# First attention of a two-layer macaron block: the own values' first block in three rounded passes instead of one fp32 product, with some products at the start and end of the stage put in another order

## The reference, cut to what matters

```python
x = x + 0.5 * ffn0(layernorm(x))
x = x + attn0(layernorm(x))            # the stage that is changed
x = x + 0.5 * ffn0(layernorm(x))
x = x + 0.5 * ffn1(layernorm(x)); x = x + attn1(layernorm(x)); x = x + 0.5 * ffn1(layernorm(x))

# attn0: 32 query heads of 128, 8 shared key/value heads, and 32 "latent" keys and values of their own
q  = rope(x @ w_q);  k = rope(x @ w_k) # k, v: one for each group of 4 query heads
v  = x @ w_v
lk = rope((x @ w_lq) @ w_lk);  lv = x @ w_lv     # one for each query head
attn = softmax(mask(q k^T / sqrt(128))) v        # over the shared keys
lat  = softmax(mask(q lk^T / sqrt(128))) lv      # over the head's own keys
return attn @ w_o + lat @ w_lo
```

## Time and profile before

| what | us |
|---|---|
| median of 3 runs | 1792.02 (1790.3 to 1793.99) |
| the profiled execution | 1789.53 |
| its span, first to last instruction | 1787.7 |
| PE busy | 1726.3 (97%) |
| DVE busy | 1169.4 (65%) |
| ACT busy | 1075.1 (60%) |
| POOL busy | 916.4 (51%) |
| first attention, about | 92 to 1347 |
| one group of 16 steps inside it | 154.3 |
| own product: L1141 and L1143 busy | 77.1 and 49.1 |

### The profile page before, as it was taken

One profiled execution on the slowest core, in us unless ns is written; L12 is line 12 of the kernel. 1 busy time (PEld: TensorE's weight loads), 2 busy tenths in 40 slices (PEclk: granted clock), 3 DMA queues, 4 the chain that ended last, 5 costly groups with the idle time before them and its releaser, 6 DMA issues.

```text
span 1787.7 us, 32013 instructions
## 1 busy us (share of the span) xinstructions
PE 1726.3 (97%) x10988; PEld 1501.7 (84%) x10988; DVE 1169.4 (65%) x3498; ACT 1075.1 (60%) x3013; POOL 916.4 (51%) x1169
## 2 busy tenths in 40 slices
PE   7989999999999999999999999999999998899798
PEld 6788999998998999899899899989878776677567
DVE  6675566566557656755665665676566676888756
ACT  3356656566656666655665664666553264888964
POOL 4555545455544555554555554545532255877850
PEclk9999999999999999999999999999999999999999
DMA  4300011012001101200110110020021121000101
GB/s 145 110 24 13 15 58 42 1 42 61 13 19 54 42 1 48 65 1 19 56 40 1 60 54 1 19 72 24 1 65 54 42 59 48 2 2 2 42 7 48
DMA packets 35424, 65.77 MB, mean 37 GB/s; under 512 B 4032, under 2 KB 4672, under 8 KB 35264
## 3 DMA queue, kind: packets, MB, share of 16 engines
q1 hardware_dynamic: 35264, 63.73, 11.6%
HBM read 61.62 MB, written 2.10 MB: 36 GB/s over the span
## 4 chain that ended last, share of the span: by engine, by line
PE 69%; ACT 11%; DVE 10%; issue 6%; POOL 3%; DMA 1%; SPq 0%; DVEq 0%; POOLq 0%; ACTq 0%
PE bank L367 57%; PE bank L1118 4%; ACT s L1264 2%; PE bank L1141 2%; PE bank L1752 2%; ACT W L263 1%; PE bank L1143 1%; DVE h L765 1%; PE bank L1723 1%; DVE work L1376 1%; DVE W L269 1%; ACT s L1818 1%; DVE work L1367 1%; PE bank L1739 1%; ACT qk L1255 1%
## 5 line engine op out<-in xcount | busy, mean ns | idle before, releaser
L1505 POOL TENSOR_TENSOR qk<-work,qk 128x512 fp32r<-128x512 f32 (+1 forms) x160 | 188.7, 1179 | 474.8 <-ACT qk L1255 474.7
L1497 POOL TENSOR_TENSOR work<-work,table 128x512 f32<-128x512 f32 (+1 forms) x160 | 190.0, 1187 | 110.5 <-ACT work L1250 110.4
L1264 ACT ACTIVATE s<-s,neg_max 128x128 f32<-128x128 f32 (+1 forms) x512 | 228.0, 447 | 1.9 <-DVE neg_max L1390 1.9
L1271 ACT CAST pt_pair<-bank 128x384 fp32r<-128x384 f32 x128 | 61.8, 482 | 249.3 <-PE bank L1118 249.3
L367 PE MATMUL bank<-W,o_own 128*128 128x512 f32 x768 | 200.6, 396 | 0.0
L1255 ACT CAST qk<-work 128x512 fp32r<-128x512 f32 (+1 forms) x160 | 92.5, 578 | 178.9 <-DVE work L1376 178.9
L367 PE MATMUL bank<-W,xnA 128*128 128x320 f32 (+1 forms) x1056 | 195.5, 339 | 3.4 <-DVE xnA L352 2.6
L367 PE MATMUL bank<-W,o_pair 128*128 128x512 f32 x768 | 197.5, 399 | 0.0
L1367 DVE TENSOR_TENSOR work<-bank,table 128x512 f32<-128x512 f32 (+1 forms) x160 | 101.9, 637 | 130.6 <-ACT work L1250 128.7
L367 PEld LDWEIGHTS bank<-W,xnA 128*128 128x128 f32 x1056 | 166.1, 189 | 17.6 <-DVE xnA L352 3.7
L367 PE MATMUL bank<-qk 128*128 128x256 f32 (+1 forms) x768 | 166.1, 352 | 0.9 <-POOL qk L1505 0.9
(11 more groups left out here) (124 smaller groups left out, 3801.9 us busy)
## 6 DMA issues: line engine op xcount, KB each, us to landing
raw<-in_weights SPq DMA_DIRECT2D x215, 256.0 KB, 2.7
x<-in_x SPq DMA_DIRECT2D x8, 256.0 KB, 6.1
out<-x SPq DMA_DIRECT2D x8, 256.0 KB, 2.0
row<-in_bias_rows SPq DMA_DIRECT2D x5, 256.0 KB, 2.9
table<-in_constants SPq DMA_DIRECT2D x4, 240.0 KB, 3.2
b_qk<-in_bias_rows SPq DMA_DIRECT2D x1, 512.0 KB, 3.9
b_val<-in_bias_rows SPq DMA_DIRECT2D x1, 256.0 KB, 3.0
table<-in_constants SPq DMA_DIRECT2D x1, 66.0 KB, 2.5
```

Source lines behind the costliest of these rows:

```text
L1264: last = nc.scalar.activation(s0[:, s, cols], s0[:, s, cols], ACT.Exp, bias=neg_max[:, s, qt:qt + 1], scale=-1.0, accum_out=row_sum[:, s, ...
L1271: nc.scalar.copy(pt_pair[HI][:, before.h % 2, :, :].rearrange("p b q -> p (b q)"), bank[PT][:, 0:3 * P]).then_inc(a_pt_hi, 1)
L1497: nc.gpsimd.tensor_tensor(work[:, s, cols], work[:, s, cols], table[:, T_SIN + cols.start:T_SIN + cols.stop], ALU.mult).then_inc(a_sin, 1)
L1505: nc.gpsimd.tensor_tensor(lo, work[:, 2 + s, st.columns(what)], hi.bitcast(F32), ALU.subtract).then_inc(a_rope_lo, 1)
```

## The change

1. The values and the weights of the first key block (256 columns of `pt_own`, the first token tile of the own values) are now held as HI and LO parts (`v_front`, `pt_front`) and multiplied by `product` in three fp32r passes. The second block (128 columns) stays one fp32 matmul (`v_rear`, `pt_rear`).
2. ACT's one copy of 384 columns becomes a cast of 256 (`pt_front` HI) and a copy of 128 (`pt_rear`); DVE gets a new instruction, `turned_own_lo`, that makes the LO part of `pt_front` and only then raises `a_pt_own`.
3. On DVE the values of the first token tile are cast and subtracted for all 640 columns instead of being copied for 512 and split for 128.
4. `v_rear` is the tile `row`, so SP's load of the bias row waits for X2, the end of the attention, and with it what stands behind it in the queue.
5. On PE the second half of the latent query projection (`other_half`: 12 products of 512 columns) goes ahead of the own product in step 1; in the last group, steps 14 to 16, `output` products go ahead of `weigh_pair` and of `turn(1)`.

```diff
@@ -171,10 +171,12 @@
                 qk = [sb(s, f"qk{i}", [P, 6, SEQ], F32R) for i in (HI, LO)]
-                lvv = sb(s, "lvv", [P, 2, GH * HD])
-                vs = [sb(s, f"vs{i}", [P, 2, HD], F32R) for i in (HI, LO)]
+                v_front = [sb(s, f"v_front{i}", [P, LVW], F32R) for i in (HI, LO)]
+                v_rear = row
+                vs_rear = [sb(s, f"vs_rear{i}", [P, HD], F32R) for i in (HI, LO)]
                 pt_pair = [sb(s, f"pt_pair{i}", [P, 2, 3, P], F32R) for i in (HI, LO)]
-                pt_own = sb(s, "pt_own", [P, 3 * P])
+                pt_front = [sb(s, f"pt_front{i}", [P, 2 * P], F32R) for i in (HI, LO)]
+                pt_rear = sb(s, "pt_rear", [P, P])
                 o_pair = [sb(s, f"o_pair{i}", [P, 2, SEQ], F32R) for i in (HI, LO)]
...
@@ -1044,8 +1047,8 @@
             turn_tiles((4, 5))
-            a0_run(pe, lambda st: a0_tensor_step(pe, st, lambda: turn_tiles((6, 7))), lambda: None,
-                   other_half)
+            a0_run(pe, lambda st: a0_tensor_step(pe, st, lambda: turn_tiles((6, 7)), other_half),
+                   lambda: None, lambda: None)
 
...
@@ -1138,9 +1141,9 @@
 
-                nc.tensor.matmul(bank[OB][:, 0:SEQ], lvv[:, 0, col:col + P], pt_own[:, 0:2 * P],
-                                 start=True, stop=False)
-                nc.tensor.matmul(bank[OB][:, P:SEQ], lvv[:, 1, col:col + P], pt_own[:, 2 * P:3 * P],
+                product(bank[OB][:, 0:SEQ], lambda p: v_front[p][:, col:col + P],
+                        lambda p: pt_front[p][:, :], True, False)
+                nc.tensor.matmul(bank[OB][:, P:SEQ], v_rear[:, col:col + P], pt_rear[:, :],
                                  start=False, stop=True).then_inc(a_pv_own, 1)
@@ -1173,22 +1176,28 @@
                 output(0, st.near(-3))
+            if not st.queries and st.h in (0, 2):
+                output(1, st.near(-2))
             if lag1 and before.paired():
                 weigh_pair()
                 turn(1)
             if st.queries and not st.first:
                 a0_queries(pe, st)
+            if not st.queries and st.h == 3:
+                output(0, st.near(-3))
             if lag1 and not before.paired():
                 turn(1)
+            if st.second and not st.first:
+                latent()
             for t in next_norms(st):
                 if t == 0:
                     pe.wait_ge(a_proj_free, st.near(-1).fill("q")[0] + 3)
                 ln_turn(pe, 16 + t, t, t % 2, normed, banks=2)
-            if lag2 and st.h in (1, 3):
+            if lag2 and (st.h == 1 or st.h == 3 and st.queries):
                 output(0, st.near(-3))
             if lag2 and st.h == 1:
                 output(0, st.near(-2))
-            if lag2 and st.h != 1:
+            if lag2 and (st.h == 3 or st.h != 1 and st.queries):
                 output(1, st.near(-2))
@@ -1273,7 +1282,8 @@
                 act.wait_ge(a_turned, before.inst(1)[0] + 1)
-                nc.scalar.copy(pt_own[:, :], bank[PT][:, 0:3 * P]).then_inc(a_pt_own, 1)
+                nc.scalar.copy(pt_front[HI][:, :], bank[PT][:, 0:2 * P])
+                nc.scalar.copy(pt_rear[:, :], bank[PT][:, 2 * P:3 * P]).then_inc(a_own_pt_hi, 1)
 
@@ -1403,6 +1413,11 @@
 
+            def turned_own_lo():
+                dve.wait_ge(a_own_pt_hi, before.number() + 1)
+                nc.vector.tensor_tensor(pt_front[LO][:, :], bank[PT][:, 0:2 * P], pt_front[HI][:, :].bitcast(F32),
+                                        ALU.subtract).then_inc(a_pt_own, 1)
+
             def pair_lo():
@@ -1419,16 +1434,23 @@
                 dve.wait_ge(a_proj, f + 1)
-                if half == 0:
-                    nc.vector.tensor_copy(lvv[:, tt, 0:HALF], bank[fs][:, 0:HALF]).then_inc(a_proj_free, 1)
-                    return
                 own = GH * HD - HALF
-                shared = bank[fs][:, own:HALF]
-                nc.vector.tensor_copy(vs[HI][:, tt, :], shared).then_inc(a_v_hi, 1)
-                nc.vector.tensor_copy(lvv[:, tt, HALF:GH * HD], bank[fs][:, 0:own])
-                dve.wait_ge(a_v_hi, st.values_before() + tt + 1)
-                nc.vector.tensor_tensor(vs[LO][:, tt, :], shared, vs[HI][:, tt, :].bitcast(F32),
-                                        ALU.subtract).then_inc(a_proj_free, 1)
+                if tt == 0:
+                    cols = slice(half * HALF, (half + 1) * HALF)
+                    hi, lo = [v_front[p][:, cols] for p in (HI, LO)]
+                    nc.vector.tensor_copy(hi, bank[fs][:, 0:HALF]).then_inc(a_v_hi, 1)
+                    dve.wait_ge(a_v_hi, st.values_before() + half + 1)
+                    nc.vector.tensor_tensor(lo, bank[fs][:, 0:HALF], hi.bitcast(F32),
+                                            ALU.subtract).then_inc(a_proj_free, 1)
+                elif half == 0:
+                    nc.vector.tensor_copy(v_rear[:, 0:HALF], bank[fs][:, 0:HALF]).then_inc(a_proj_free, 1)
+                else:
+                    shared = bank[fs][:, own:HALF]
+                    nc.vector.tensor_copy(vs_rear[HI][:, :], shared).then_inc(a_v_hi, 1)
+                    nc.vector.tensor_copy(v_rear[:, HALF:GH * HD], bank[fs][:, 0:own])
+                    dve.wait_ge(a_v_hi, st.values_before() + 3)
+                    nc.vector.tensor_tensor(vs_rear[LO][:, :], shared, vs_rear[HI][:, :].bitcast(F32),
+                                            ALU.subtract).then_inc(a_proj_free, 1)
 
@@ -1450,6 +1472,8 @@
                 inverses(1)
+            if lagging(st):
+                turned_own_lo()
             for t in next_applied(st):
@@ -2135,7 +2159,7 @@
                 st_tail.load(sp, j, flat(W_F1 - len(TAIL) + j))
-            sp.wait_ge(x_written, X1)
+            sp.wait_ge(x_written, X2)
             sp.dma_start(row[:, :], rows_in[0]).then_inc(row_loaded, 16)
```

More of the change, by code:

```diff
@@ L907, in program @@
         a_pt_own = sem("a_pt_own")
+        a_own_pt_hi = sem("a_own_pt_hi")
         a_pt_hi = sem("a_pt_hi")
@@ L946, in values_before @@
             def values_before(self):
-                return 2 * (self.g * BATCH + self.batch)
+                return 3 * (self.g * BATCH + self.batch)
             def paired(self):
@@ L1093, in score_columns, with a0_tensor_step @@
             return bank[2 + qt][:, (1 - k) * n:(2 - k) * n]
-        def a0_tensor_step(pe, st, between):
+        def a0_tensor_step(pe, st, between, latent):
             def scores():
@@ L1125, in weigh_pair @@
                 to = bank[OB][:, :].rearrange("p (e q) -> p e q", e=2)
-                product(to, lambda p: vs[p][:, 0, :],
+                product(to, lambda p: v_front[p][:, GH * HD:LVW],
                         lambda p: pt_pair[p][:, :, 0:2, :].rearrange("p e b q -> p e (b q)"), True, False)
-                product(to[:, :, P:SEQ], lambda p: vs[p][:, 1, :],
+                product(to[:, :, P:SEQ], lambda p: vs_rear[p][:, :],
                         lambda p: pt_pair[p][:, :, 2, :], False, True).then_inc(a_pv_pair, 1)
```

## The result

| | us |
|---|---|
| before, median of 6 | 1792.53 |
| after, median of 6 | 1799.32 (1796.72 to 1799.96) |
| ratio, 95% interval | 1.0037 (1.0025 to 1.0048) |
| profiled execution (span) before, after | 1789.53 (1787.7), 1798.65 (1796.9) |

It is slower by 6.8 us; the forecast was 1795.3, 2.8 slower on the median and 3.3 on the profiled pair, where 9.2 were found. The sign and the places are as forecast, the size is not.

What follows compares the result with a forecast made beforehand. PE, busy 97% of the span, was taken to bound the kernel. Regular groups +4.7, last group +1.0, start -1.9, end -0.5 gave +3.3 us: 1792.8 profiled, 1795.3 on the median; range 1790 to 1799, 8 in 10 1784 to 1802.

Steps and rivals of the forecast that it cites:

- The sign: Whole kernel against the kernel before: slower had a chance of 0.40, same 0.38, faster 0.22.
- this account: The main forecast for the whole kernel, 1795.3 on the median, chance 0.55, its own range 1790 to 1799.
- PE saves 0.07 a head: Own product's 256 columns on PE: three fp32r passes take 0.36 instead of 0.43 us, saving 1.12 per group.
- `a_pt_own` comes 0.53 later; waits at positions 2, 6, 10, 13 and 14: Own product's operand comes later; the five positions cost 0.64, 0.28, 0.27, 0.35 and 0.48 us in a regular group.
- my own three terms, 0.10, 0.03 and 0.42: Delay of `a_pt_own`: ACT ends 0.10 later, DVE needs 0.03 to see it and 0.42 us to subtract.
- Key steps: the rotation comes 0.69 later: DVE at positions 1, 5, 9, 13: subtraction ahead of the keys' rotation delays it 0.69 us and pushes later heads.
- Last group +1.0: Last group: normalisation stands behind the subtraction and positions 8 to 10 lack slack; +1.0 us, between 0.5 and 2.
- Start -1.9: Step 1: 12 latent products fill PE's idle time, 2.4 us shorter, about 0.5 eaten by positions 1 and 2.
- The larger work on the values: DVE's 320-column subtractions fall where DVE waits for PE: nothing, at most 0.5 us per sequence, 16.
- End -0.5, row 0: Moved output products give -0.5 us, between +0.5 and -3.6; the later row load costs nothing unless landing takes twice as long.
- "Passes simply saved": Rival, chance 0.20: in the regular groups the waits hide and PE's saving is kept, 1779 to 1783 us.
- "New step dearer": Rival, chance 0.18: ACT's copies don't overlap, subtraction meets POOL, `a_pt_own` comes 0.75 later; 1808 us, half way 1802.

Runs made afterwards that it cites:

- wait_only: Kernel before, own product still fp32, with ACT's copy in two pieces and an unused subtraction on DVE that the own product waits for: 1808.92 us, ratio 1.0094.
- key_first: Changed kernel, but in the key steps DVE rotates the keys before making the low part of the own weights: 1787.24 us, ratio 0.9969.
- the ends alone: Kernel before with only PE's new order at the start and end of the stage, own product in fp32, no subtraction: 1788.08 us, ratio 0.9976.
- values_behind: key_first with DVE copying the last 128 columns and, in the first step, making the reciprocals ahead of the first half of the values: 1779.14 us, ratio 0.9924.
- row_late: Kernel before with one edit, the bias row loaded behind the attention (X2) instead of ahead of it: 1792.88 us, ratio 1.0002.

## Why the prediction was right in sign and short in size

On the median 6.8 us were measured against 2.8 forecast. The sign was a weak hit: slower had a chance of 0.40, the same 0.38. And 1799.3 lies at the edge of the 1790 to 1799 that I gave to this account; only the wider range, which reaches towards the rivals, holds it with room. By its own steps, on the profiled pair (+9.2 measured, +3.3 forecast):

- *PE saves 0.07 a head.* Right as a price (0.35 against 0.43), wrong as income: I took 1.12 per group, and got 0.53, since steps that end in a wait don't give theirs. Part of that loss was in the forecast: its terms for positions 2, 6 and 10 each hold 0.07 because PE comes earlier, so it counted on 0.91.
- *`a_pt_own` comes 0.53 later; waits at positions 2, 6, 10, 13 and 14.* Right, at those five and no other in a regular group. The delay itself is 0.51 (ACT ends 0.05 later, not 0.10); my own three terms, 0.10, 0.03 and 0.42, add up to 0.55 and not to the 0.53 that I wrote. The price of all waits was 1.79 in the forecast, or 1.58 without the three 0.07 of an earlier PE, which wait_only doesn't have; wait_only shows 1.85. That hides errors of both signs. Positions 6 and 10 cost 0.50 each with what follows, not 0.21; positions 2 and 3 cost 0.43, not 0.57; and the pair product gives back 0.37 at 15, where I had 0.23, at position 0 and for another reason.
- *Key steps: the rotation comes 0.69 later.* This is the term that was mis-sized. The rotation begins 0.66 later, counted from the start of ACT's copy, but takes 0.73 instead of 0.44, since it meets POOL; I had priced it as if nothing stood beside it. The miss per group is 0.65, and positions 6, 7, 10 and 11 hold all of it (0.93 against 0.27), 0.33 for each of the two key steps, close to the rotation's 0.3: 4.6 us in seven groups, of the 5.9 that the forecast fell short. At the other positions too high a price and too high an income nearly cancel, which is luck. key_first shows that the order on DVE is the cause: with it a group is 1.56 shorter. It doesn't part the push from the meeting.
- *Last group +1.0.* 1.4 from position 1 to 12; its normalisation, now behind the subtraction too, takes 0.73 instead of 0.53 beside the same POOL instruction.
- *Start -1.9.* -1.6. The new order alone does more than I said: step 1 is 2.86 shorter instead of 2.4, 0.46 of it is eaten at position 2, and 2.3 is kept. But in the changed kernel the first own product comes 1.04 later against the stage's first rotation, where 0.46 was forecast and the ends alone show 0.13. The larger work on the values, which I had at nothing, has a part in that; values_behind shows that moving the reciprocals ahead of it doesn't win it back.
- *End -0.5, row 0.* -0.3 and 0.
- *The rivals.* "Passes simply saved" is wrong: no position without slack was spared. "New step dearer" is wrong in its mechanism (0.425 for the subtraction, `a_pt_own` 0.51 later and not 0.75); its time half way, 1802, came nearer than my 1795.3, since another instruction became dearer by the same neighbour.
- *From the profile to the median.* The pair differs by 9.2, the medians by 6.8. Part may be the clock at the start (below); the stages behind the attention vary between executions of one kernel (the two profiles of the kernel before part by 1.9 us there). The split stays open.

## What to carry to other kernels

When an instruction is pushed to a later time on VectorE, price not only the push but its new neighbour: here an instruction with two SBUF operands that landed near the start of a GpSimd instruction waited it out (0.73 instead of 0.42). Put what another engine waits for ahead of a new instruction, not behind it. A saving on the busiest engine counts only in the stretches that this engine bounds; find these by the waits in the timeline, and in the others shorten the chain instead (here one copy moved from ScalarE to VectorE was worth 0.51 a group, the passes 0.66).

## What the runs showed of the hardware

PE's clock at the start. PE's idle time of 2.5 to 3 us ahead of the first own product is in five profiled kernels or executions, and in three of them the granted clock then fell. Windows 112 to 122 and 122 to 132, the last numbers being clock, DMA share and GB/s; row_late, then wait_only, then the kernel with the ends alone, where the idle time is filled:

```profile
112.00:122.00 10.00, 7.53 (x37) 6.33 (x36) 4.82 (x17) 4.46 (x14) 4.40 (x6) 0.83 0.00 0
122.00:132.00 10.00, 10.00 (x70) 9.16 (x69) 6.89 (x19) 7.90 (x22) 5.04 (x8) 1.00 0.04 8
```
```profile
112.00:122.00 10.00, 7.03 (x36) 6.03 (x35) 5.92 (x20) 4.84 (x15) 4.39 (x6) 0.78 0.00 0
122.00:132.00 10.00, 10.00 (x59) 8.68 (x57) 4.69 (x17) 5.64 (x18) 3.60 (x6) 0.88 0.00 0
```
```profile
112.00:122.00 10.00, 10.00 (x67) 9.05 (x66) 7.39 (x25) 5.93 (x17) 4.46 (x6) 1.00 0.00 0
122.00:132.00 10.00, 9.89 (x67) 8.88 (x66) 7.78 (x25) 8.46 (x24) 6.77 (x9) 1.00 0.19 54
```

A mean between 0.5 and 1 is part of the window at 1.2 GHz and the rest at 2.4. In row_late the step took 1.57 us longer for it than in the shown profile of the kernel before: the 12 products of the projection behind the first own product take 4.42 there (117.92 to 122.34), where the earlier trace rows has 2.86. From the mean of 0.83 over these 10 us an estimate of the loss is 1.7 us. All nine profiles in which the idle time is filled have 1.00 in both windows. So the new start order keeps 2.3 us and, in some executions, saves this drop besides. That would fit the median of the ends alone (-4.7) beside its stage (-3.1, against a profile without the drop), but the profiles are too few to show it.
